# Token mixing with three spatial pieces in each spectral step in place of two

## The chip, the cores and the metric

The kernel runs on one core of a Trainium2 chip. The metric is the device time of one execution in microseconds (us); the time given for a version is the median over its runs.

## The reference

The input is an image tensor of shape 4 x 32 x 128 x 128: four batches of 32 tokens, each a 128 x 128 picture. Layer 0 is an attention over tokens whose keys, queries and values are made by spectral convolutions. The part that matters here is how the attention weights are applied and projected back to one channel:

```
dprod = softmax(einsum('bhtd,bhsd->bhts', qf, kf) / scale)      # 16 heads, 32 x 32 weights in each batch
attn  = einsum('bhts,bhsd->bhtd', dprod, vf)                    # mixes the tokens of a batch, head by head
attn  = fno_layer(attn, proj_w, proj_skip_w, proj_skip_b, (H, W))   # 16 heads -> 1 channel:
                                                                # a spectral part (34 x 17 low modes) and a 1x1 skip part
attn  = instance_norm(attn + tokens, ...)
```

After it come a mixer with two more spectral layers, an attention over 4,096 positions in each of four sequences, and a mixture of eight experts with a residual. These later parts are the bulk of the time and are not touched.

## The kernel before

The program is a row of stages, each a block that all five engines enter and leave together: an engine that is done with a stage waits at its end for the others. The stage of this change is `stage_mix`. It computes the attention product and the projection above in two independent forms:

- The **spectral** part. The 578 complex low modes of the tokens are cut into five tiles (`MT`: four of 128 modes, one of 66), and the 16 heads into four groups of four (q = 0 to 3). This gives 20 `steps` (k, q). In a step TensorE (PE) multiplies the real and the imaginary modes by the attention weights (two matmuls at L909, called **the pair** here, into PSUM banks 0 to 5 in turn, so that three steps fit). VectorE (DVE) makes three weighted products of the result (L972), and ScalarE (ACT) the fourth (L934, four instructions). GpSimd (POOL) joins them (L993, L994). When the four steps of a tile are summed, DVE reduces over the heads (L961, two instructions); this reduction stands in DVE's queue after the step with q = 1 of the next tile, so after steps 5, 9, 13 and 17, and the last one at the end.
- The **spatial** part. The skip part mixes whole pictures, cut into `NCH` = 32 **pieces** of 512 pixels-by-token columns. A piece is one matmul (L900, `spatial(n)`) into bank 6 or 7, and one ScalarE instruction that scales it, adds the offset and writes it back over the pictures (L941). Once all 32 are written, SyncE (SP) sends the pictures to memory in four transfers (L952), from which the next stage reads them.

Nothing depends on how the two parts are interleaved but the queues. The order in them is written out in the code: in each step the pair comes first, then the pieces of that step; ScalarE's queue has the four L934 of the step first and then its pieces. Semaphores tie the queues together:

- `spatial(n)` waits until piece n-2 has been written back (`added`), since both use one bank.
- DVE's first product of step i waits for the pair (`xm`); ScalarE's L934 of step i waits for that first product (`odd`); L941 waits for the piece's matmul (`mixed`).
- The pair of step i waits until DVE and ScalarE are done with step i-3 (`used`, `scaled`).
- DVE and ScalarE wait in step i until POOL has summed step i-4 (`summed`); a reduction waits until POOL has summed its tile.

After the steps, PE transposes the reduced modes (L921), ScalarE copies them (L946), and DVE forms coefficients from them (L1002 to L1005); that ends the stage. The next stage, `stage_inverse` of kind 'proj', starts with loads of the mixed pictures (L1120).

Of the kernel before, what the change touches and what calls it, by code (L numbers as in the profile page):

```python
# [151 lines left out]
def reached(eng, sem, value):  # L152

    if not (isinstance(value, int) and value <= 0):
        eng.wait_ge(sem, value)


def over(ap, axis, n):

    shape = list(ap.shape)  # L160
    return ap.unsqueeze(axis).to_broadcast(shape[:axis] + [n] + shape[axis:])


def semaphores(nc, held, stage, names):

    made = {n: nc.alloc_semaphore(f"{stage}_{n}") for n in names.split()}
    held.extend(made.values())
    return Names(made)
# [612 lines left out]
def weight_views(m):  # L781
    w = Views()
    w.sum = m.wk[:, 0:240].rearrange("p (k h) -> p k h", k=5)
    big = [m.wk[:, 240 + 80 * i:320 + 80 * i].rearrange("p (k h) -> p k h", k=5) for i in range(9)]
    w.ar, w.ai, w.an, w.ur, w.ui, w.t1, w.t2, w.t3, w.t4 = big
    w.cg, w.cm = m.wk[:, 960:976], m.wk[:, 976:992]

    w.r1, w.mix, w.mixT = m.wk[:, 640:656], m.wk[:, 656:688], m.wk[:, 688:720]
    return w
# [87 lines left out]
def stage_mix(nc, held, m, mix):  # L877


    s = semaphores(nc, held, "mix", "v mixed added stored xm odd used scaled summed free reduced turned copied low kept summed_up offset")  # L880
    w = weight_views(m)
    NCH = PIX // 512
    LOWS = [(0, 512), (512, 1024), (1024, FM * FM)]
    f0, f1 = (v.rearrange("p x y -> p (x y)") for v in (m.feat0, m.feat))
    steps = [(k, q) for k in range(len(MT)) for q in range(4)]

    with nc.Block() as block:
        @block.tensor
        def _(pe):
            pe.matmul(m.ps[7][:, 0:1], m.mixA, m.unity[:, 0:1], start=True, stop=True).then_inc(s.summed_up, 1)  # L890
            for i, (lo, hi) in enumerate(LOWS):
                pe.matmul(m.ps[4 + i][:, 0:hi - lo], m.mixA, f0[:, lo:hi], start=True, stop=True).then_inc(s.low, 1)

            def spatial(n):
                reached(pe, s.added, n - 1)
                if n == 0:
                    pe.wait_ge(s.kept, len(LOWS))
                if n == 1:
                    pe.wait_ge(s.offset, 1)
                pe.matmul(m.ps[6 + n % 2], m.mixA, m.a[:, :, 4 * n:4 * n + 4], start=True, stop=True).then_inc(s.mixed, 1)  # L900

            for i, (k, q) in enumerate(steps):
                m0, n = MT[k]
                if i == 2:
                    pe.wait_ge(s.kept, len(LOWS))
                reached(pe, s.used, i - 2)
                reached(pe, s.scaled, i - 2)
                for part in (0, 1):
                    mm = pe.matmul(m.ps[2 * (i % 3) + part][0:n, :], m.modes[:, part, m0:m0 + n],  # L909
                                   m.probT[:, 4 * q:4 * q + 4, :], start=True, stop=True)  # L910
                mm.then_inc(s.xm, 1)
                for j in range(2 * i, min(2 * i + 2, NCH)):
                    spatial(j)
            for k, (m0, n) in enumerate(MT):
                pe.wait_ge(s.reduced, k + 1)
                if k == 0:
                    pe.wait_ge(s.used, len(steps))
                    pe.wait_ge(s.scaled, len(steps))
                reached(pe, s.copied, k - 2)
                for part in (0, 1):  # L920
                    mm = pe.transpose(m.ps[k % 3][:, part * P:part * P + n], m.modesT[0:n, k, part, :], m.ident[0:n, 0:n])  # L921
                mm.then_inc(s.turned, 1)

        @block.scalar
        def _(act):
            for i, (lo, hi) in enumerate(LOWS):
                act.wait_ge(s.low, i + 1)
                act.copy(f1[:, lo:hi], m.ps[4 + i][:, 0:hi - lo]).then_inc(s.kept, 1)
            for i, (k, q) in enumerate(steps):
                n = MT[k][1]  # L930
                act.wait_ge(s.odd, i + 1)
                reached(act, s.summed, i - 3)
                for h in range(4):
                    o = act.activation(m.zprod[i % 4][0:n, 3, h, :], m.ps[2 * (i % 3) + 1][0:n, h * P:h * P + P], ACT.Copy,  # L934
                                       scale=w.ur[0:n, k, 4 * q + h:4 * q + h + 1])
                o.then_inc(s.scaled, 1)
                for j in range(2 * i, min(2 * i + 2, NCH)):
                    act.wait_ge(s.mixed, j + 1)
                    if j == 0:
                        act.wait_ge(s.offset, 1)  # L940
                    act.activation(m.a[:, :, 4 * j:4 * j + 4], m.ps[6 + j % 2].rearrange("p (h w) -> p h w", w=4), ACT.Identity,  # L941
                                   scale=m.rstd[:, j:j + 1], bias=m.norms[0][:, j:j + 1]).then_inc(s.added, 1)
            for k, (m0, n) in enumerate(MT):
                act.wait_ge(s.turned, k + 1)
                src = m.ps[k % 3][:, 0:2 * P].rearrange("p (c n) -> p c n", c=2)[:, :, 0:n]
                act.copy(m.modes[:, :, m0:m0 + n], src).then_inc(s.copied, 1)  # L946

        @block.sync
        def _(sp):
            for q in range(4):  # L950
                sp.wait_ge(s.added, NCH)
                sp.dma_start(mix[:, 32 * q:32 * q + 32, :], m.a[:, 32 * q:32 * q + 32, :]).then_inc(s.stored, 16)  # L952
            sp.wait_ge(s.stored, 64)

        @block.vector
        def _(vec):
            def reduce(k):
                n = MT[k][1]
                vec.wait_ge(s.summed, 4 * k + 4)
                for part in (0, 1):  # L960
                    e = vec.tensor_reduce(m.modesT[0:n, k, part, :], m.zsum[k % 2][0:n, part], AX.X, ALU.add)  # L961
                e.then_inc(s.reduced, 1)

            vec.wait_ge(s.summed_up, 1)
            vec.tensor_scalar(m.norms[0], m.back, m.ps[7][:, 0:1], None, ALU.mult).then_inc(s.offset, 1)
            for i, (k, q) in enumerate(steps):
                n = MT[k][1]
                vec.wait_ge(s.xm, i + 1)
                reached(vec, s.summed, i - 3)
                for j, part, u in ((1, 1, w.ui), (0, 0, w.ur), (2, 0, w.ui)):  # L970
                    src = m.ps[2 * (i % 3) + part][0:n, :].rearrange("p (h t) -> p h t", h=4)
                    ins = vec.tensor_tensor(m.zprod[i % 4][0:n, j], src, over(u[0:n, k, 4 * q:4 * q + 4], 2, P), ALU.mult)  # L972
                    if j == 1:
                        ins.then_inc(s.odd, 1)
                ins.then_inc(s.used, 1)
                if k and q == 1:
                    reduce(k - 1)
            reduce(len(MT) - 1)
            vec.wait_ge(s.reduced, len(MT))
            vec.wait_ge(s.copied, len(MT))  # L980
            form_coefficients(vec, m, m.modes[:, 0], m.modes[:, 1])

        @block.gpsimd
        def _(pool):
            for i, (k, q) in enumerate(steps):
                n = MT[k][1]
                pool.wait_ge(s.used, i + 1)
                pool.wait_ge(s.scaled, i + 1)
                if q == 0:
                    reached(pool, s.reduced, k - 1)  # L990
                re, im = (m.zsum[k % 2][0:n, part, :, 4 * q:4 * q + 4].rearrange("p t h -> p h t") for part in (0, 1))
                z = m.zprod[i % 4]
                pool.tensor_tensor(re, z[0:n, 0], z[0:n, 1], ALU.subtract)  # L993
                pool.tensor_tensor(im, z[0:n, 2], z[0:n, 3], ALU.add).then_inc(s.summed, 1)  # L994
# [1634 lines left out]
```

## Time and profile before

| what | value |
|---|---|
| time before, median of 3 runs | 2350.61 us (2346.66 to 2353.24) |
| the profiled execution's own time | 2354.32 us |
| span of the profiled execution | 2352.4 us |
| PE busy | 2082.6 us, 89% of the span |
| DVE busy | 1882.0 us, 80% |
| ACT busy | 1665.1 us, 71% |
| POOL busy | 602.9 us, 26% |
| matmuls of the pieces (L900) | first at 150.1 us, last at 212.4 us |

How to read it: the span is the time between the first and the last instruction that the profiler saw, and the time of an execution is a little above it. The busy shares are means over all stages; the stage of this change takes under a twentieth of the span, so its own rows have to be read. A matmul in float32 stands in the trace as two instructions, so the pair of a step is four rows of PE, and a piece two.

### The profile page before, as it was taken

To read this page: it belongs to the slowest core of one execution; us is meant where nothing else is said; L and a number is where in the kernel's file an instruction comes from. 1 tells how busy PE (TensorE), PEld (TensorE's weight loads), DVE (VectorE), ACT (ScalarE), POOL (GpSimd) and SP (SyncE) were. 2 spreads that over 40 slices of the span, in tenths; PEclk is the share of its full clock that TensorE was granted. 3 is DMA by queue.
4 is the path that set the end of the run, shared out by engine and by line. 5 is a ranking of instruction groups with operands and counts; after the bars stand their busy time and mean duration, and the time that the engine had idled before them with its cause. 6 is when DMAs were issued, how large, how long until landed. Compare 5 with 4: busy or idle time off the path is not lost. (4 is left out here: it accounts for less than half of the span.)

```text
span 2352.4 us, 30833 instructions
## 1 busy us (share of the span) xinstructions
PE 2082.6 (89%) x10374; PEld 1067.8 (45%) x10374; DVE 1882.0 (80%) x3586; ACT 1665.1 (71%) x2413; POOL 602.9 (26%) x750
## 2 busy tenths in 40 slices
PE   7767859865899999999999999999999999767778
PEld 7722437732444444444444444444444444333333
DVE  4666887688778889889888888889888888867776
ACT  1444236464778888888888888878888888667666
POOL 1035415335302202102102102112000001046668
PEclk9978655555999999999999999999999999889999
DMA  9003560000000000000000000000000000000101
GB/s 301 9 1 143 153 151 3 1 1 6 1 10 1 1 1 1 1 1 1 1 1 1 1 1 1 1 1 1 1 1 1 1 1 1 0 14 28 32 28 46
DMA packets 80833, 55.72 MB, mean 24 GB/s; under 512 B 11283, under 2 KB 78739, under 8 KB 79140
## 3 DMA queue, kind: packets, MB, share of 16 engines
q1 hardware_dynamic: 75476, 52.38, 7.4%
q10 hardware_dynamic: 5200, 1.38, 0.3%
q8 instruction: 82, 1.34, 0.2%
q14 instruction: 75, 0.61, 0.1%
HBM read 36.91 MB, written 16.78 MB: 23 GB/s over the span
## 5 line engine op out<-in xcount | busy, mean ns | idle before, releaser
L2004 ACT ACTIVATE inner<-banks,key_bias,scales 128x1024 f32<-128x1024 f32 x512 | 617.2, 1205 | 212.5 <-PE banks L1821 207.3
L2189 DVE TENSOR_TENSOR weights_low<-weights,weights_high 128x1024 f16<-128x1024 f32 x512 | 674.4, 1317 | 17.0
L2011 ACT ACTIVATE weights<-inner 128x1024 f32<-128x1024 f32 x512 | 541.1, 1057 | 17.3 <-DVE weights_low L2189 1.6
L2185 DVE CAST weights_high<-weights 128x1024 f16<-128x1024 f32 x512 | 371.3, 725 | 175.8 <-ACT weights L2011 161.6
L2295 POOL CAST sums_high<-sums 128x512 f16<-128x512 f32 x32 | 39.1, 1221 | 1089.2 <-ACT sums L1983 1071.3
L1821 PE MATMUL banks<-queries_high,keys_high 128*128 128x512 f16 x1024 | 304.5, 379 | 0.7 <-ACT inner L2004 0.7
L1836 PE MATMUL banks<-weights_high,tokens_low 128*128 128x512 f16 x1024 | 304.6, 379 | 0.0
L1821 PE MATMUL banks<-queries_low,keys_high 128*128 128x512 f16 x1024 | 304.6, 379 | 0.0
L1821 PE MATMUL banks<-queries_high,keys_low 128*128 128x512 f16 x1024 | 304.6, 379 | 0.0
L1836 PE MATMUL banks<-weights_low,tokens_high 128*128 128x512 f16 x1024 | 304.6, 379 | 0.0
L1836 PE MATMUL banks<-weights_high,tokens_high 128*128 128x512 f16 x1024 | 304.5, 379 | 0.0
L2494 ACT ACTIVATE scaled<-banks,gates 128x128 f32<-128x128 f32 x512 | 149.2, 395 | 88.6 <-PE banks L2456 88.5
L1836 PEld LDWEIGHTS banks<-weights_high,tokens_low 128*128 128x128 f16 x1024 | 100.2, 98 | 120.9
L1821 PEld LDWEIGHTS banks<-queries_low,keys_high 128*128 128x128 f16 x1024 | 100.2, 98 | 120.9
L1836 PEld LDWEIGHTS banks<-weights_low,tokens_high 128*128 128x128 f16 x1024 | 100.2, 98 | 120.8
L1821 PEld LDWEIGHTS banks<-queries_high,keys_low 128*128 128x128 f16 x1024 | 100.2, 98 | 120.8
L1836 PEld LDWEIGHTS banks<-weights_high,tokens_high 128*128 128x128 f16 x1024 | 100.2, 98 | 120.8
L2454 PE MATMUL banks<-expert_weights_high,normed_high 128*128 128x512 f16 x256 | 103.3, 403 | 57.0 <-DVE residual_and_scaled L2530 43.7
L1821 PEld LDWEIGHTS banks<-queries_high,keys_high 128*128 128x128 f16 x1024 | 96.8, 98 | 91.3 <-ACT inner L2004 1.7
L2559 POOL TENSOR_TENSOR scaled_halves<-scaled 128x256 f32<-128x256 f32 x128 | 94.9, 741 | 93.4 <-ACT scaled L2494 93.0
L2530 DVE SCALAR_TENSOR_TENSOR residual_and_scaled<-banks,gates,residual_and_scaled 128x128 f32<-128x128 f32 x384 | 109.9, 341 | 0.1
L2455 PE MATMUL banks<-expert_weights_low,normed_high 128*128 128x512 f16 x256 | 103.2, 403 | 0.0
(613 smaller groups left out, 3243.0 us busy)
## 6 DMA issues: line engine op xcount, KB each, us to landing
images_b<-in_x SPq DMA_DIRECT2D x32, 256.0 KB, 9.4
images_a<-in_x SPq DMA_DIRECT2D x8, 1024.0 KB, 9.8
mixed_scratch<-images_a SPq DMA_DIRECT2D x4, 2048.0 KB, 13.1
result<-group_result SPq DMA_DIRECT2D x32, 256.0 KB, 2.3
images_b<-mixed_scratch SPq DMA_DIRECT2D x10, 768.0 KB, 5.2
images_a<-in_x SPq DMA_DIRECT2D x10, 768.0 KB, 9.1
mixer_weights<-in_L_conv_mixer_w SPq DMA_DIRECT2D x4, 272.0 KB, 6.8
table<-tables ACTq DMA_DIRECT2D x1, 772.5 KB, 7.1
```

The costliest lines, as they stand in the source:

```text
L1821: mm = pe.matmul(m.ps[2 * (t % 2) + h], key[:, par, part], query[:, q, 512 * h:512 * h + 512], start=(i == 0), stop=(i == 2))
L1836: mm = pe.matmul(m.ps[4 + h], value[:, par, k, :], weight[:, t % DEEP, 512 * h:512 * h + 512], start=(k == 0 and i == 0), stop=(k == KT - ...
L2004: act.activation(m.inner[:, t % 2, :], m.pair[t % 2], ACT.Exp, scale=m.fs[:, 1:2], bias=m.kb[:, c // QN % 2, k:k + 1]).then_inc(s.inner, 1)
L2011: act.activation(m.wt[:, t % 2, :], m.inner[:, t % 2, :], ACT.Exp).then_inc(s.outer, 1)
L2185: vec.tensor_copy(m.wH[:, t % DEEP, :], m.wt[:, t % 2, :]).then_inc(s.high, 1)
L2189: vec.tensor_tensor(m.wL[:, t % DEEP, :], m.wt[:, t % 2, :], m.wH[:, t % DEEP, :], ALU.subtract)\
L2295: after(pool.tensor_copy(m.oH[:, part], m.oS[:, part]))
L2454: pe.matmul(bank, m.lnH[:, t % RING, j, :], m.w8H[:, cols], start=True, stop=False)
L2455: pe.matmul(bank, m.lnH[:, t % RING, j, :], m.w8L[:, cols], start=False, stop=False)
L2494: o = act.activation(m.pb[:, n % 3, e, :], m.ps[ABANK[n % 2]][:, e * D:e * D + D], ACT.Copy, scale=m.gate[:, n, 4 + e:5 + e])
L2530: vec.scalar_tensor_tensor(out=m.u[:, n % 4, :], in0=m.ps[DBANK[n % 3]][:, e * D:e * D + D], scalar=m.gate[:, n, e:e + 1], in1=acc, op0=AL ...
L2559: pool.tensor_tensor(m.half[:, n % 2], m.pb[:, n % 3, 0:2], m.pb[:, n % 3, 2:4], ALU.add).then_inc(s.halved, 1)
```

## The change

The two loops that say which pieces follow a step, one in PE's queue and one in ScalarE's, take three pieces for each step in place of two. With 32 pieces, steps 0 to 9 now have three, step 10 has two, and steps 11 to 19 have none; before, steps 0 to 15 had two and steps 16 to 19 none.

```
@@ stage_mix, PE's queue
                 mm.then_inc(s.xm, 1)
-                for j in range(2 * i, min(2 * i + 2, NCH)):
+                for j in range(3 * i, min(3 * i + 3, NCH)):
                     spatial(j)
@@ stage_mix, ScalarE's queue
                 o.then_inc(s.scaled, 1)
-                for j in range(2 * i, min(2 * i + 2, NCH)):
+                for j in range(3 * i, min(3 * i + 3, NCH)):
                     act.wait_ge(s.mixed, j + 1)
```

The queues of DVE, POOL and SP hold the same instructions in the same order. On PE, at the start of the steps, this stood before (L909 is the pair, from the modes in `modes` and the weights in `images_b`; L900 a piece, from the pictures `images_a`; in brackets what it waits for):

```order
L909 MATMUL banks<-images_b,modes 128x512 x2
L900 MATMUL banks<-images_a,transposed 128x512 [waits mix_kept]
L900 MATMUL banks<-images_a,transposed 128x512 [waits mix_offset]
L909 MATMUL banks<-images_b,modes 128x512 x2
L900 MATMUL banks<-images_a,transposed 128x512 [waits mix_added] x2
```

and this stands there now:

```order
L909 MATMUL banks<-images_b,modes 128x512 x2
L900 MATMUL banks<-images_a,transposed 128x512 [waits mix_kept]
L900 MATMUL banks<-images_a,transposed 128x512 [waits mix_offset]
L900 MATMUL banks<-images_a,transposed 128x512 [waits mix_added]
L909 MATMUL banks<-images_b,modes 128x512 x2
L900 MATMUL banks<-images_a,transposed 128x512 [waits mix_added] x3
```

The third piece of a step, number 3i+2, waits for the write-back of the step's own first piece, 3i. With two pieces to a step each piece waited for one of the step before.

On ScalarE, at the start of the steps, this stands now (L934 is the fourth product, four instructions, the first of which waits for DVE's first product; L941 is the write-back of a piece):

```order
L934 ACTIVATE images_b<-banks,images_b 128x128 [waits mix_odd]
L934 ACTIVATE images_b<-banks,images_b 128x128 x3
L941 ACTIVATE images_a<-banks,norms 128x128x4 [waits mix_offset,mix_mixed]
L941 ACTIVATE images_a<-banks,norms 128x128x4 [waits mix_mixed] x2
L934 ACTIVATE images_b<-banks,images_b 128x128 [waits mix_odd]
L934 ACTIVATE images_b<-banks,images_b 128x128 x3
L941 ACTIVATE images_a<-banks,norms 128x128x4 [waits mix_mixed] x3
```

All write-backs of a step, the first piece's too, stand behind the step's four L934. That was so before as well, with two write-backs.

On PE, from step 10 (the first pair shown) to step 15, the difference reads (banks_0 to banks_2 are the pairs of PSUM banks that the steps use in turn, banks_3 is banks 6 and 7):

```order
 L909 MATMUL banks_1<-images_b,modes 128x512 x2
 L900 MATMUL banks_3<-images_a,transposed 128x512 x2
 L909 MATMUL banks_2<-images_b,modes 128x512 x2
-L900 MATMUL banks_3<-images_a,transposed 128x512 x2
 L909 MATMUL banks_0<-images_b,modes 128x512 x2
-L900 MATMUL banks_3<-images_a,transposed 128x512 x2
 L909 MATMUL banks_1<-images_b,modes 128x512 x2
-L900 MATMUL banks_3<-images_a,transposed 128x512 x2
```

From step 11 on the pairs follow each other with no piece between them.

## Rows read from the trace of the kernel before

**Rows 1.** The profile page: busy time (share of the span) and instructions of each engine.

```profile
PE 2082.6 (89%) x10374; PEld 1067.8 (45%) x10374; DVE 1882.0 (80%) x3586; ACT 1665.1 (71%) x2413; POOL 602.9 (26%) x750
```

**Rows 2.** Windows over the stage: us, busy PE, PEld, DVE, ACT, POOL; clock, DMA, GB/s.

```profile
150.00:160.00 10.00, 10.00 (x24) 4.37 (x23) 5.66 (x9) 7.03 (x18) 5.83 (x5) 1.00 0.00 0
...
190.00:200.00 10.00, 8.06 (x15) 3.33 (x15) 5.20 (x9) 6.58 (x17) 5.38 (x5) 0.83 0.00 1
...
210.00:220.00 10.00, 10.00 (x20) 3.22 (x20) 5.65 (x9) 5.33 (x15) 7.00 (x7) 0.83 0.50 210
220.00:230.00 10.00, 2.35 (x9) 1.49 (x8) 6.95 (x8) 3.75 (x12) 7.00 (x6) 0.69 1.04 442
```

**Rows 3.** Timeline of the first steps: start, length, engine, line, operation, [idle before <-releaser].

```profile
148.16 2.14 PE L909 MATMUL banks<-images_b,modes 128*128 128x512 f32 x4
...
150.35 1.89 DVE L972 TENSOR_TENSOR images_b<-banks,images_b 128x512 f32<-128x512 f32 x3 [5.75 <-PE banks L909]
...
155.29 1.88 PE L909 MATMUL banks<-images_b,modes 128*128 128x512 f32 x4
...
157.21 1.89 DVE L972 TENSOR_TENSOR spare<-banks,images_b 128x512 f32<-128x512 f32 x3 [1.55 <-PE banks L909]
157.94 1.14 ACT L934 ACTIVATE spare<-banks,images_b 128x128 f32<-128x128 f32 x4 [0.95 <-DVE spare L972]
...
158.73 1.88 PE L909 MATMUL banks<-images_b,modes 128*128 128x512 f32 x4
...
158.96 1.47 ACT L941 ACTIVATE images_a<-banks,norms 128x512 f32<-128x512 f32 x2
```

**Rows 4.** Timeline around the first reduction, after step 5.

```profile
167.51 1.89 DVE L972 TENSOR_TENSOR images_b<-banks,images_b 128x512 f32<-128x512 f32 x3 [1.55 <-PE banks L909]
...
169.31 4.47 DVE L961 TENSOR_REDUCE transposed<-images_b 128x128 f32<-128x2048 f32 x2
...
173.70 3.67 DVE L972 TENSOR_TENSOR spare<-banks,images_b 128x512 f32<-128x512 f32 x6
...
175.43 1.47 ACT L941 ACTIVATE images_a<-banks,norms 128x512 f32<-128x512 f32 x2
...
175.70 1.29 POOL L993 TENSOR_TENSOR features<-spare 128x512 f32<-128x512 f32 x1 [3.65 <-DVE spare L972]
176.28 1.98 PE L900 MATMUL banks<-images_a,transposed 128*128 128x512 f32 x4 [1.94 <-ACT images_a L941]
...
178.17 1.29 POOL L993 TENSOR_TENSOR features<-spare 128x512 f32<-128x512 f32 x1
```

**Rows 5.** Timeline of PE alone, after the first, second and third reduction.

```profile
178.10 1.88 PE L909 MATMUL banks<-images_b,modes 128*128 128x512 f32 x4
179.82 1.88 PE L900 MATMUL banks<-images_a,transposed 128*128 128x512 f32 x4
...
192.22 2.99 PE L900 MATMUL banks<-images_a,transposed 128*128 128x512 f32 x4 [1.94 <-ACT images_a L941]
...
197.46 1.88 PE L900 MATMUL banks<-images_a,transposed 128*128 128x512 f32 x4
...
209.86 3.56 PE L900 MATMUL banks<-images_a,transposed 128*128 128x512 f32 x4 [1.94 <-ACT images_a L941]
213.21 2.04 PE L909 MATMUL banks<-images_b,modes 128*66 128x512 f32 x4
```

**Rows 6.** Timeline of the end of the stage.

```profile
213.46 0.78 ACT L941 ACTIVATE images_a<-banks,norms 128x512 f32<-128x512 f32 x1 [0.93 <-PE banks L900]
...
223.28 3.67 DVE L972 TENSOR_TENSOR spare<-banks,images_b 66x512 f32<-66x512 f32 x6
...
236.83 0.45 DVE L1005 SCALAR_TENSOR_TENSOR pair<-modes 128x289 f32<-128x289 f32 x1
```

**Rows 7.** Waits of SP's queue at the end of the stage: total, times, longest.

```profile
SPq L887 <- PEq L887: 2.0, 1, 2.0
```

**Rows 8.** A window of 20 us in the expert stage, columns as in rows 2.

```profile
2170.00:2190.00 20.00, 16.74 (x110) 8.51 (x108) 13.65 (x47) 19.47 (x64) 15.64 (x31) 1.00 0.09 27
```

More of the change, by code:

```diff
@@ L911, in _ @@
                 mm.then_inc(s.xm, 1)
-                for j in range(2 * i, min(2 * i + 2, NCH)):
+                for j in range(3 * i, min(3 * i + 3, NCH)):
                     spatial(j)
@@ L936, in _ @@
                 o.then_inc(s.scaled, 1)
-                for j in range(2 * i, min(2 * i + 2, NCH)):
+                for j in range(3 * i, min(3 * i + 3, NCH)):
                     act.wait_ge(s.mixed, j + 1)
```

## The prediction

> **What bounds the kernel now.** I read the page first: PE is busy for 89% of the span [rows 1], but that is a mean over twelve stages, nearly all of it from the long attention. So I went to windows of 10 us over the stage of the change, then to its timeline, engine by engine. Two different regimes are to be seen. At 150 to 160 us PE is busy for all 10.00 us while DVE has 5.66, ACT 7.03 and POOL 5.83 [rows 2]: here PE sets the pace. At 220 to 230 us PE has 2.35, and DVE and POOL about 7 each [rows 2]: here PE hardly matters.
>
> The steady step is 3.44 us long (a pair at 155.29, the next at 158.73 [rows 3]), of which the pair takes 1.72 (178.10 to 179.82 [rows 5]) and two pieces the other 1.72, so 0.86 for a piece. DVE needs only 1.80 for its three products (167.51 to 169.31) [rows 4]. The reductions break this: DVE is held for 4.39 us (169.31 to 173.70), ACT's products queue behind it and its write-backs behind those, and PE idles 1.94 us before its next piece [rows 4]. The same 1.94 comes after the second and third reduction [rows 5], and after these two the matmuls also run slower for a while: piece pair and pair take 5.24 us (192.22 to 197.46) where 3.54 (176.28 to 179.82) was enough the first time, and two pieces 3.35 (209.86 to 213.21) in place of 1.82 [rows 4, 5]. The windows show a granted clock of 1.00 at 150 to 160 us, but 0.83 at 190 to 200 and at 210 to 220 us, so parts of these were at the lower level, 1.2 GHz [rows 2]. They cost 1.70 and 1.53 us, 3.2 together.
>
> The end of the stage hangs on DVE. Its products of steps 18 and 19 start at 223.28, a last reduction follows, then the transposes and coefficients, and the stage's last instruction ends at 237.28, 14.0 us after 223.28 [rows 6]. SP, which leaves the stage only when its transfers have landed, then waited 2.0 us more for the others [rows 7], so the pictures were 2 us early. The start of DVE's step 18 is therefore what I follow through the change: 223.28 now.
>
> **The change part by part.** No instruction is added or removed; 32 pieces are 32 pieces, and DVE, POOL and SP keep their queues. What changes is which wait stands where.
>
> *A new wait in steps 0 to 9.* The third piece of a step waits for the write-back of the step's first piece. That write-back stands behind ACT's four products, which wait for DVE, which waits for the pair. From the start of the pair: 1.92 us to DVE's start (155.29 to 157.21), 0.73 to ACT's products (157.94), 1.02 to its write-back (158.96) [rows 3], 0.85 from a write-back's start to the piece that waits for it (175.43 to 176.28) [rows 4]. Sum 4.52. PE reaches the third piece at 1.72 + 2 x 0.86 = 3.44 and so idles about 1.08. The piece after an idle time costs a little more: two took 1.82 (176.28 to 178.10) [rows 4, 5], so I put the first at 0.96. A step with three pieces then takes 4.52 + 0.96 = 5.48 us, not 1.72 + 3 x 0.86 = 4.30. Queued behind the waiting piece is the next pair, and all of DVE, ACT and POOL wait for that. The bounds of this term: 4.30 below, if the wait never shows; 5.48 as summed, where every link is a row. I take 5.48, since the code leaves no way round the chain.
>
> *The reductions in steps 0 to 10.* After step 5, DVE's products and reduction end 1.92 + 1.80 + 4.39 = 8.11 us after that step's pair [rows 3, 4]; step 6's products could have begun at 5.48 + 1.92 = 7.40. So 0.71 late instead of PE's 1.94 before: the longer step hides most of it. After step 9 DVE is 0.71 late as well, but step 10 has only two pieces, so PE doesn't feel that.
>
> *Steps 0 to 10 together.* The first pair starts at 148.16 and its products at 150.35, which is 2.19 and not 1.92, so 0.27 for the start [rows 3]. The pair of step 10: 148.16 + 0.27 + 10 x 5.48 + 0.71 = 203.94. DVE's step 10: 203.94 + 1.92 + 0.71 = 206.57, done at 208.37. The pair of step 11, two pieces later: 203.94 + 3.44 = 207.38; DVE's step 11 at 209.30.
>
> *Steps 11 to 19 without pieces.* Now PE needs 1.72 a step and DVE 1.80, so DVE sets the pace; the PE time that pieces could have filled is idle. DVE: step 12 at 211.10, step 13 at 212.90, reduction from 214.70 (POOL takes about 2.47 a step, 175.70 to 178.17 [rows 4], so has summed step 11 by 213.9), 219.09 after it, four steps of 1.80 to 226.29, reduction to 230.68. POOL has summed step 15 by then: it can start on step 14 at 221.0 and needs two steps, 225.9, just in time. DVE's step 18 starts at 230.7 against 223.28: 7.4 us late. From there on the instructions are those of before, and the 14.0 us to the end stay.
>
> *The stores.* The last write-back, number 31, now stands in step 10: DVE at 206.57, ACT's products 0.73 later, its two write-backs 1.02 after that, the second one 0.74 (half of 1.47 [rows 3]) later still: 209.1, against 213.46 [rows 6]. SP's transfers then land about 4.4 us earlier. They were 2 us early already [rows 7], so that is worth nothing; the cover is DVE's own tail, and it grows.
>
> *The low clock.* Before, 3.2 us of the stage were lost at it. By the same count a run of before without these losses would be 3.2 us shorter, and then the change costs 10.6. In the changed kernel the idle time is 1.08 in each 5.48, and its matmuls run for four fifths of the time. In the expert stage PE is busy for 16.74 of 20 us and the granted clock is 1.00, the level of 2.4 GHz [rows 8]. So I expect the full clock to hold in steps 0 to 9. PE will idle for longer during the reductions after steps 13 and 17, but what follows there has DVE to wait for anyway.
>
> **The sum.** Against the profiled execution: 2354.32 + 7.4 = 2361.7. That execution was 3.7 us above the median of 2350.61, and part of this may be the low-clock loss that other runs have less of. So against the median I take between 7.4 and 10.6, nearer to the former: +8.4, 2359.0 us. About 0.3%, 7.05 us, is what a measurement of this kernel tells from no change; the forecast lies just beyond it.
>
> **The rivals.**
> 1. *The forecast*: the wait inside the step, at full clock. 2354 to 2362. Chance 0.76.
> 2. *The repeated short idle times pull the clock down* in the changed kernel. For it speaks that two of three idle times of 1.94 us were followed by slow matmuls [rows 5]; against it that the first wasn't [rows 4], that the new ones are half as long, and the expert stage's 1.00 [rows 8]. A fall cost 1.6 us on average. Five of them in the ten steps make +8 on top: 2367; one in each step makes 2375. It decides from about one fall in each two steps. Chance 0.14. The Trainium skill, "TensorE: Matmul & The Clock Gate", section "A second HAM failure mode: psum-queue depth-cycling", says that a PE which idles shortly and often between groups of matmuls can swing between its two clock levels; by that rule this rival would come about, and the trace of before agrees in part, with two slow stretches in three.
> 3. *The wait inside the step doesn't bite*, as the chain is shorter than I add it up, and PE's gain shows: the 10 steps take 4.30 each. A reduction then makes DVE 8.11 - 6.22 = 1.89 late, and step 10's pair comes at 148.16 + 0.27 + 43.0 + 1.9 = 193.3, DVE's step 10 at 197.1 instead of 206.57, all 9.5 earlier: 2349.5, not slower. The point from which it decides is a step of 5.48 - 0.84 = 4.64 us. Against it stands that every link of 4.52 is read from a row. Chance 0.06.
> 4. *The stores end the stage*, so that issuing them 4.4 us earlier brings the end forward by as much: 2350.6 - 4.4 = 2346.2. For it speaks only that they land within 2 us of the end; against it that SP then waited for the others [rows 7]. Chance 0.04.
>
> **How the numbers follow.** The range reaches from 2352 to 2368: it holds the forecast's own 2354 to 2362 and more than half of rival 2, and leaves out rivals 3 and 4 and the costly half of 2. Beyond +7.05 lie rival 2 (0.14) and some 0.48 of the forecast's 0.76: slower 0.62. Within 0.3% lie the other 0.28 of it and most of rivals 3 and 4: same 0.34. For faster 0.04 is left, the edge of rival 4 and of rival 3 if step 10 comes earlier than I have it.
>
> **What would show it.** In the changed timeline: PE rows of L900 with some 1.08 us of idle time before each third piece, released by ACT's L941; DVE's products 5.5 us apart in steps 0 to 9, and 1.80 apart from step 11; the stage's last L1005 ending near 244.7, not 237.28; SP's transfers issued near 210; granted clock 1.00 from 150 to 205. Steps near 4.3 us would show rival 3, longer rows of L900 and L909 (0.43 us a part is full clock) rival 2. I would be wrong, too, if the 3.2 us of low clock in this one execution of before are untypical: then the sign stays, and the size moves by as much.

## The result and the profile after

The changed kernel takes 2359.55 us in the median of six runs (2356.71 to 2363.0), against 2350.84 us for the kernel before, also six runs: a ratio of 1.0038, with a 95% interval from 1.0026 to 1.0049. It is slower by 8.7 us, with an interval from 6.1 to 11.5; the forecast was 2359.0.

The profiled execution has a span of 2357.6 us. On the page, the busy times have hardly moved:

```profile
span 2357.6 us, 30833 instructions
...
PE 2077.8 (88%) x10374; PEld 1065.6 (45%) x10374; DVE 1883.0 (80%) x3586; ACT 1665.8 (71%) x2413; POOL 602.4 (26%) x750
```

As many instructions, as busy as before [rows 1]: what was added is waiting. PE's timeline of the changed kernel, from step 1 to step 3, shows where (L909 is the pair, L900 the pieces; the last entry is the idle time before the row and what ended it):

```profile
152.38 1.88 PE L909 MATMUL banks<-images_b,modes 128*128 128x512 f32 x4
154.10 1.88 PE L900 MATMUL banks<-images_a,transposed 128*128 128x512 f32 x4
156.89 1.13 PE L900 MATMUL banks<-images_a,transposed 128*128 128x512 f32 x2 [0.91 <-ACT images_a L941]
157.85 1.88 PE L909 MATMUL banks<-images_b,modes 128*128 128x512 f32 x4
159.57 1.88 PE L900 MATMUL banks<-images_a,transposed 128*128 128x512 f32 x4
162.36 1.12 PE L900 MATMUL banks<-images_a,transposed 128*128 128x512 f32 x2 [0.91 <-ACT images_a L941]
163.32 1.88 PE L909 MATMUL banks<-images_b,modes 128*128 128x512 f32 x4
```

Each step's third piece stands alone in a row, behind 0.91 us of idle time that a write-back of ScalarE ends. From pair to pair it is 5.47 us (152.38 to 157.85). The links of the chain can be read on ScalarE in the same step:

```profile
155.02 1.14 ACT L934 ACTIVATE images_b<-banks,images_b 128x128 f32<-128x128 f32 x4 [1.67 <-DVE images_b L972]
156.04 1.47 ACT L941 ACTIVATE images_a<-banks,norms 128x512 f32<-128x512 f32 x2
158.05 0.78 ACT L941 ACTIVATE images_a<-banks,norms 128x512 f32<-128x512 f32 x1 [0.55 <-PE banks L900]
```

ScalarE's products start 2.64 us after the pair (155.02 less 152.38), its write-back 3.66 us and the third piece 4.51 us after it. DVE's timeline shows the first reduction, the passage to the steps without pieces, and the end:

```profile
176.19 1.89 DVE L972 TENSOR_TENSOR images_b<-banks,images_b 128x512 f32<-128x512 f32 x3 [3.58 <-PE banks L909]
177.99 4.47 DVE L961 TENSOR_REDUCE transposed<-images_b 128x128 f32<-128x2048 f32 x2
182.38 1.88 DVE L972 TENSOR_TENSOR spare<-banks,images_b 128x512 f32<-128x512 f32 x3
187.84 1.89 DVE L972 TENSOR_TENSOR spare<-banks,images_b 128x512 f32<-128x512 f32 x3 [3.58 <-PE banks L909]
...
204.97 1.88 DVE L972 TENSOR_TENSOR spare<-banks,images_b 128x512 f32<-128x512 f32 x3
207.68 1.89 DVE L972 TENSOR_TENSOR spare<-banks,images_b 128x512 f32<-128x512 f32 x3 [0.84 <-PE banks L909]
209.49 3.67 DVE L972 TENSOR_TENSOR images_b<-banks,images_b 128x512 f32<-128x512 f32 x6
213.08 4.47 DVE L961 TENSOR_REDUCE transposed<-images_b 128x128 f32<-128x2048 f32 x2
217.46 3.67 DVE L972 TENSOR_TENSOR spare<-banks,images_b 128x512 f32<-128x512 f32 x6
221.05 3.66 DVE L972 TENSOR_TENSOR images_b<-banks,images_b 66x512 f32<-66x512 f32 x6
224.63 4.46 DVE L961 TENSOR_REDUCE transposed<-features 128x128 f32<-128x2048 f32 x2
229.02 3.66 DVE L972 TENSOR_TENSOR spare<-banks,images_b 66x512 f32<-66x512 f32 x6
...
242.56 0.46 DVE L1005 SCALAR_TENSOR_TENSOR pair<-modes 128x289 f32<-128x289 f32 x1
```

Up to step 9 DVE waits 3.58 us for the pair in each step but the one right behind the first reduction. In step 11 it waits 0.84 us, and from there to step 19 for no pair at all: it alone sets the pace. Its step 18 starts at 229.02 against 223.28 before [rows 6]. The stage began a little earlier in this execution, with its first pair at 146.69 against 148.16 [rows 3], so from here on I count from the first pair: step 18 at 82.33 us against 75.12, the end of the last coefficients at 96.33 against 89.12 (the prediction had it at 244.7, which is 96.5 after its first pair). That is 7.2 us. SP's waits at the end of the stage:

```profile
SPq L887 <- DMA mixed_scratch<-images_a: 18.4, 1, 18.4
SPq L887 <- PEq L887: 13.3, 1, 13.3
```

The pictures were sent earlier, and SP then waited 13.3 us for the others where it had waited 2.0 [rows 7].

### The profile page after: what moved, and what is told of

The parts are those of the page before. It is cut to its first block and busy times, and to the rows that moved or that the text cites. A ratio compares the mean times of both kernels' runs of the same rounds, so it can differ in the third digit from the quotient of the medians.

```text
span 2357.6 us, 30833 instructions
## 1 busy us (share of the span) xinstructions
PE 2077.8 (88%) x10374; PEld 1065.6 (45%) x10374; DVE 1883.0 (80%) x3586; ACT 1665.8 (71%) x2413; POOL 602.4 (26%) x750
```

## The experiments

Below, "ahead" says how many write-backs of a step's own pieces stand in front of its four products in ScalarE's queue. It was none in both kernels. The experiments that need it use one edit, with the write-back as a function, shown here against the changed kernel. Their line numbers are shifted by it (L933 is the write-back, L978 DVE's products, L967 its reduction, L958 the transfers):

```
             for i, (k, q) in enumerate(steps):
...
+                for j in own[:ahead]:
+                    write_back(j)
                 act.wait_ge(s.odd, i + 1)
                 (the step's four products)
                 o.then_inc(s.scaled, 1)
-                for j in range(3 * i, min(3 * i + 3, NCH)):
-                    (wait for the piece, write it back)
+                for j in own[ahead:]:
+                    write_back(j)
```

**Three pieces, the first write-back ahead.** `own` is the three pieces of the step, `ahead` is 1.

> Three pieces to a step as in the change, but in ScalarE's queue the write-back of a step's first piece stands ahead of the step's four products, so that the third piece no longer waits for a chain over VectorE. Theory A (the wait inside the step is the price): steps 0 to 9 take about 4.4 us in place of 5.47, the idle time before each third piece falls from 0.91 us to under 0.3, VectorE's step 18 starts about 72 us after the first pair in place of 82.3, and the time falls by about 10 us to 2349, at or a little under that of before. Theory B (the price lies in the late steps left without pieces, wherever the waits are): VectorE's step 18 stays near 82 us after the first pair, and the time near 2359.

Measured: 2349.67 us, ratio 0.9994 to the kernel before (0.9985 to 1.0003). From PE's timeline:

```profile
149.04 2.29 PE L909 MATMUL banks<-images_b,modes 128*128 128x512 f32 x4
151.17 3.02 PE L900 MATMUL banks<-images_a,transposed 128*128 128x512 f32 x6
154.02 1.88 PE L909 MATMUL banks<-images_b,modes 128*128 128x512 f32 x4
155.74 3.02 PE L900 MATMUL banks<-images_a,transposed 128*128 128x512 f32 x6
158.59 1.88 PE L909 MATMUL banks<-images_b,modes 128*128 128x512 f32 x4
```

The three pieces now run as one row, and the step is 4.57 us (154.02 to 158.59), somewhat over the 4.4 expected and 0.27 over the 4.30 that a pair and three pieces take without a wait. The rest is a shorter wait: the third piece shares its bank with the first, so it waits for the first one's write-back wherever that stands in ScalarE's queue. ScalarE and the loads of the pieces (PEld, the weight loads of PE) show it, and DVE's step 18 follows:

```profile
156.79 0.78 ACT L933 ACTIVATE images_a<-banks,norms 128x512 f32<-128x512 f32 x1 [1.42 <-PE banks L900]
...
157.62 0.30 PEld L900 LDWEIGHTS banks<-images_a,transposed 128*128 128x128 f32 x2 [0.84 <-ACT images_a L933]
...
222.15 3.67 DVE L978 TENSOR_TENSOR spare<-banks,images_b 66x512 f32<-66x512 f32 x6
```

DVE's step 18 starts 73.1 us after the first pair, 9.2 sooner than with the change. So the wait for the chain over DVE is there; moving one instruction takes away 0.90 of the 1.17 us by which it made each step longer than 4.30. That gives back all that the change cost. It does not yet say that the wait is the whole cause, since the kernel before had waits of its own.

**Four pieces to a step.** The same edit as the change, with 4 in place of 3.

> Four pieces to a step, steps 0 to 7, and twelve steps without any. Theory A: still one wait inside a step, since the fourth piece's write-back is ready by then, so a step takes 5.47 + 0.86 = 6.33 us, there are eight of them, and the reduction after step 5 is hidden whole: VectorE's step 18 some 83.5 us after the first pair, 1.2 us later than with three; about 2361. Theory B: the price goes with the steps without pieces (4 before, 9 with the change, 12 here), 7.2 us for the first five, so 11.5 us above before: VectorE's step 18 at 86.6, about 2364.

Measured: 2359.52 us, ratio 1.0038 (1.0025 to 1.0051), as the change itself. The steps are 6.33 us long, as theory A has it; here are the idle times of two neighbours on PE:

```profile
154.28 1.98 PE L900 MATMUL banks<-images_a,transposed 128*128 128x512 f32 x4 [0.92 <-ACT images_a L941]
160.61 1.98 PE L900 MATMUL banks<-images_a,transposed 128*128 128x512 f32 x4 [0.91 <-ACT images_a L941]
```

Step 18 starts 84.97 us after the first pair (227.38 less 142.41), where A gave 83.5 and B 86.6, and 1.0 of it came from a slow first step (2.94 us from the first pair to DVE's start at 145.35, against 1.92). The time is nearer to A's 2361 than to B's 2364. The price does not grow with the number of steps left without pieces alone.

**The kernel before, both write-backs ahead.** Two pieces to a step, `ahead` is 2.

> The kernel before, two pieces to a step, with both write-backs of a step ahead of its four products in ScalarE's queue. Theory A (it is ScalarE's queue that carries VectorE's delays to PE): the three idle times of 1.94 us after reductions vanish, the low-clock stretches behind them as well, and VectorE's step 18 starts about 65 us after the first pair in place of 75.1; the time falls by some 9 to 10 us, to 2341. Rival: the four products come later in their step and GpSimd's sums with them, which holds VectorE instead: then step 18 stays near 75 us and the time near 2350.

Measured: 2340.18 us, ratio 0.9955 (0.994 to 0.997): 10.7 us faster than the kernel before, and the fastest of all. Around the first reduction, and at step 18, DVE's timeline now reads:

```profile
168.40 4.47 DVE L967 TENSOR_REDUCE transposed<-images_b 128x128 f32<-128x2048 f32 x2
172.78 3.67 DVE L978 TENSOR_TENSOR spare<-banks,images_b 128x512 f32<-128x512 f32 x6
176.89 1.89 DVE L978 TENSOR_TENSOR images_b<-banks,images_b 128x512 f32<-128x512 f32 x3 [0.44 <-PE banks L909]
...
212.34 3.67 DVE L978 TENSOR_TENSOR spare<-banks,images_b 66x512 f32<-66x512 f32 x6
```

The kernel before had at that third row:

```profile
180.02 1.89 DVE L972 TENSOR_TENSOR images_b<-banks,images_b 128x512 f32<-128x512 f32 x3 [2.65 <-PE banks L909]
```

PE's timeline of the new version through the same time:

```profile
169.82 1.88 PE L900 MATMUL banks<-images_a,transposed 128*128 128x512 f32 x4
171.54 1.88 PE L909 MATMUL banks<-images_b,modes 128*128 128x512 f32 x4
173.26 1.88 PE L900 MATMUL banks<-images_a,transposed 128*128 128x512 f32 x4
174.97 1.88 PE L909 MATMUL banks<-images_b,modes 128*128 128x512 f32 x4
```

PE runs through the reduction. DVE does two steps after it without waiting, as it did before, and then waits 0.44 us for the third pair in place of 2.65. Step 18 starts 64.8 us after the first pair (212.34 less 147.51). GpSimd's later sums hold none of the steps up to there: the rival has fallen.

**The kernel before once more**, for its trace.

> The kernel before once more, for its trace alone. The prediction took the two slow stretches after the second and third reduction (3.2 us together) as something that other executions may have less of. If they are typical, VectorE's step 18 is again about 75.1 us after the first pair and two or three idle times of 1.94 us are followed by matmuls at the lower clock; if they were chance, it is near 72 us.

PE after the three reductions:

```profile
170.69 1.98 PE L900 MATMUL banks<-images_a,transposed 128*128 128x512 f32 x4 [1.94 <-ACT images_a L941]
...
186.63 3.68 PE L900 MATMUL banks<-images_a,transposed 128*128 128x512 f32 x4 [1.94 <-ACT images_a L941]
...
204.26 1.98 PE L900 MATMUL banks<-images_a,transposed 128*128 128x512 f32 x4 [1.94 <-ACT images_a L941]
```

DVE's step 18:

```profile
215.99 3.67 DVE L972 TENSOR_TENSOR spare<-banks,images_b 66x512 f32<-66x512 f32 x6
```

The same three idle times, but only one is followed by slow matmuls (3.68 us for two pieces), where it was two in the first trace [rows 5]. Step 18 starts 73.15 us after the first pair (at 142.84), and the stage takes 87.1 us, 2.0 less than in the first trace. Neither of the two expectations: the loss varies from execution to execution.

**Even spread.** `own` is `range(8 * i // 5, 8 * (i + 1) // 5)` on both engines, `ahead` is 0.

> The 32 pieces spread over all 20 steps (1, 2, 1, 2, 2 and so on), products ahead of write-backs as before. This tests the fourth rival of the prediction, the transfers to memory, by making them late. Theory A: VectorE's step 18 starts about 68 us after the first pair, since PE has work to cover in each step and no step waits inside; but the last write-back starts only at 73 us, and the transfers, which landed some 22 us after it before, land at 95 us and end the stage in place of VectorE (89 before): slower by about 7, 2358. If the transfers could not end the stage: 68 + 14 = 82 us, 2345.

Measured: 2361.07 us, ratio 1.0034 (1.0023 to 1.0045); the kernel before, measured beside this and the next two, took 2352.22. Issue of the transfers, and SP's waits:

```profile
220.86 3.07 SPq L958 DMA_DIRECT2D mixed_scratch<-images_a  x4
...
SPq L887 <- DMA mixed_scratch<-images_a: 18.0, 1, 18.0
SPq L887 <- PEq L887: 0.2, 1, 0.2
```

DVE is done 85.3 us after the first pair (228.36 less 143.03), but the transfers landed at 98.9 (220.86 + 3.07 + 18.0 less 143.03), and nobody was waited for after them: here the transfers end the stage. The 73 us expected for the last write-back were 4 too early (220.06, so 77.0), and the 68 for DVE's step 18 were 3 too early (214.36, so 71.3): PE idled up to 2.79 us after reductions, and ran slowly behind three of its four idle times. The sense of the expectation holds, the size was 3 us short.

**Even spread, all write-backs ahead.** As the last, with `ahead` 2.

> The even spread and the write-backs of a step ahead of its products. VectorE's step 18 about 61 us after the first pair, its end of the stage at 75; last write-back at 63, transfers landed at 85. Theory A: the transfers end the stage, at 85 us against 87 to 89 before: 2348, so worse than two pieces a step with the same queue (2340), though VectorE is done 4 us sooner. If the transfers did not matter: 2337.

Measured: 2346.35 us, ratio 0.9981 (0.9969 to 0.9993). DVE's step 18 starts 60.5 us after the first pair (205.14 less 144.67), the transfers landed at 84.7 (208.33 + 3.07 + 18.0 less 144.67), and SP waited 0.2 us more. DVE was done 10 us earlier, at 74.5; that is lost to the transfers.

**Three pieces, all write-backs ahead.** `own` is the three pieces, `ahead` is 3.

> Three pieces to a step with all three write-backs ahead of the products: no piece waits for VectorE any more, so this leaves only the other part of the change, the steps without pieces. Against the same queue with two pieces to a step (2340.2) theory A expects PE's steps of 4.3 to 4.4 us up to step 10, VectorE waiting for pairs there, and then nine steps at VectorE's own pace with PE idle: VectorE's step 18 about 72 us after the first pair against 65, so 7 us slower, 2347. If only the waits mattered, it would be at 2340 as well.

Measured: 2349.15 us, ratio 0.9989 (0.9979 to 1.0). Against the ratio 0.9955 of two pieces with the same queue that is 0.34%, or 8 us, slower. On DVE:

```profile
165.21 1.89 DVE L978 TENSOR_TENSOR images_b<-banks,images_b 128x512 f32<-128x512 f32 x3 [2.69 <-PE banks L909]
...
194.25 3.70 DVE L978 TENSOR_TENSOR spare<-banks,images_b 128x512 f32<-128x512 f32 x6
...
217.40 3.66 DVE L978 TENSOR_TENSOR spare<-banks,images_b 66x512 f32<-66x512 f32 x6
```

DVE waits 2.7 us for the pair in the steps with three pieces (4.57 us long, by PE's rows of L909), but for the two behind the first reduction, and for no pair from step 10 on. Step 18 starts 72.4 us after the first pair (217.40 less 145.02), against 64.8. No write-back stands behind products here, yet not all of the 7.6 us is the uneven load. The steps are as long as in the first experiment, 0.27 us over 4.30, and PE's weight loads wait for ScalarE's write-backs here too (8.4 us in ten waits). Nine of these steps lie ahead of the reduction that DVE then works through, so by estimate 2.4 us are that wait for the bank, and some 5 the uneven load. No run gave the pieces a third bank, which would measure the split.

**The changed kernel once more**, for its trace.

> The changed kernel once more, for its trace alone. If the short idle times leave the clock alone, the stage is again 96.3 us from the first pair to the last coefficients, within 0.3, unlike before, whose stage was 89.1 us in one trace and 87.1 in the other.

DVE's step 18:

```profile
226.89 3.67 DVE L972 TENSOR_TENSOR spare<-banks,images_b 66x512 f32<-66x512 f32 x6
```

PE's idle times are again 0.91 us, and 1.62 in the step after the first reduction. From the first pair (144.82) to the end of the last coefficients (240.43 + 0.45) it is 96.1 us, 0.3 less than in the first trace.

## Why the prediction was right

Set side by side, the start of DVE's step 18, in us after the first pair (mean of the two traces where there are two):

| | two pieces to a step | three pieces to a step |
|---|---|---|
| products first (as in both kernels) | 74.1 | 82.2 |
| all write-backs first | 64.8 | 72.4 |

*The wait inside the step* was read off correctly: 5.47 us a step against 5.48 forecast, the third piece 4.51 us after the pair against 4.52. The idle time in the profile's sense is 0.91, not 1.08, since a row of PE ends 0.16 us after the next can start. Taking ScalarE's products out of its path is worth 9.8 us (82.2 to 72.4).

*The reductions* hide as forecast: step 6's third piece idles 1.62, that is 0.71 more than 0.91. The kernel before loses about as much to them: 9.3 us (74.1 to 64.8), with the slow stretches. So the change put one set of waits in the place of another of nearly the same size.

*What is left* is the price of three pieces with the same queue order on both sides: 8.1 us with products first, 7.6 with write-backs first. Of the 7.6, by the estimate above, 2.4 are the third piece's wait for its bank and some 5 the uneven load, with no pieces left for the late steps. Together: 9.8 + 2.4 + 5.2 added, 9.3 taken away, 8.1 net. The prediction's sum had all of this in it, step by step, but its name for the likeliest case, the wait inside the step, says too much. It is true that without that wait the change costs nothing against the kernel before (the first experiment). It is also true that the kernel before without its own waits is 8 us ahead of the change with the same order in ScalarE's queue. The second is the comparison of like with like.

*Why uneven load costs here*: PE's work is 20 pairs of 1.72 and 32 pieces of 0.86, 61.9 us; DVE's up to step 18 is 18 steps of 1.80 and four reductions of 4.39, 50.0 us. With three pieces to a step at first, DVE waits for PE in the first half and cannot make it up in the second, where PE idles. Going the other way, the even spread with write-backs first starts step 18 at 60.5 us, 4.3 sooner than two pieces to a step with the same queue.

*The stores*: issued 61.5 us after the first pair (208.19 less 146.69), against 61.8 forecast, and worth nothing, as forecast. The two even spreads show that the fourth rival was no empty one: when the last write-back comes late enough, they end the stage. In the kernel before and in its faster version they are within 2 us of it.

*The low clock* did not come to the changed kernel's steps with pieces; its windows:

```profile
150.00:160.00 10.00, 8.17 (x20) 3.25 (x18) 2.83 (x6) 6.07 (x13) 5.04 (x4) 1.00 0.00 0
160.00:170.00 10.00, 8.17 (x19) 3.25 (x18) 3.54 (x6) 6.52 (x14) 5.03 (x4) 1.00 0.00 0
...
190.00:200.00 10.00, 8.66 (x20) 3.63 (x20) 3.11 (x6) 5.58 (x12) 4.88 (x4) 1.00 0.01 2
```

The granted clock is 1.00 with PE busy for 8.17 of 10 us, so the second rival fell. The Trainium skill, "TensorE: Matmul & The Clock Gate", section "A second HAM failure mode: psum-queue depth-cycling", tells of a bf16 kernel whose short idle times between groups of matmuls made the clock swing; with float32 matmuls and 0.91 us of idle time in each 5.47, this trace does not agree. Later in the stage, after 3.23 us of idle time, twelve matmul instructions took 6.70 us where the second trace has 5.48: the low clock again (0.50 granted from 219 to 221 us), but DVE waited for no pair there, as the prediction had it.

*The size.* The prediction's sum went from 7.4 to a forecast of 8.4 on the ground that other runs of before may lose less at the low clock than the profiled one. The second trace of before agrees, with 1.7 us of such loss where the first had 3.2: the stage of before takes 89.1 and 87.1 us, that of the change 96.3 and 96.1, so the difference lies between 7.0 and 9.2, and the medians gave 8.7. That the forecast of 2359.0 came within 0.6 us of the measured 2359.55 is luck. The measured difference itself has an interval from 6.1 to 11.5 us, and what lies outside the stage took from 2258.0 to 2263.3 us in these four traces, for reasons that no run here settles.

*The third rival* needed steps under 4.64 us. Its 4.30 was reached in no run, since the wait for the bank stays in every order of ScalarE's queue. With the queue as the change has it the steps are 5.47; the first experiment shows that they would have been 4.57 had a single write-back stood elsewhere, and then the time is indeed that of before.

## What to carry to other kernels

In a queue that is filled by hand, an instruction that another engine waits for should not stand behind one that waits for a third engine: moving ScalarE's write-backs ahead of its products was worth 10.7 us here, more than any spread of the pieces. It works as long as what is pushed back holds nobody in its turn, as GpSimd's sums here. When the number of pieces to a step is changed, write down for each piece whose release it waits for: with two buffers, the third piece of a step is the first one that waits for its own step, wherever the write-back stands. Work that one engine can do at any time is best spread so that the engine next in line is fed throughout, unless a transfer hangs on its last piece.

## What the runs showed of the hardware

Idle times of 1.94 us on PE were followed by matmuls at about half speed in three cases of six (two traces of the kernel before) and in one of two in the even spread, where both idle times of about 2.8 us (2.79 and 2.77) were followed by slow ones as well. Idle times of 0.91 us in each 5.47 left the granted clock at 1.00 for 60 us (windows from 150 to 210 us, in both traces of the changed kernel). In the fastest version, whose PE runs through the reductions, the matmul instructions of the pieces all take 0.59 us, and the granted clock is 1.00 in every window from 150 to 210 us. The four transfers of 2 MB each from the pictures to memory had landed 18.0 to 18.6 us after the end of their issue in every run, wherever in the stage they stood.
